# Four-layer graph network: the loops over pairs of edge groups in the attention stage, written out as straight code on all five engines

## The chip, the core and the metric

The kernel runs on one core of one Trainium2 chip. The metric is device time in microseconds (us) from the program's start to its end. Beside it there is one profiled execution, whose rows are quoted here. In it PE is TensorE's matmul, PEld its weight load, DVE is VectorE, ACT is ScalarE, POOL is GpSimd and SP is SyncE, which here only starts transfers; a "q" behind an engine's name (DVEq, SPq) is its sequencer, which fetches and hands out the instructions.

## What is computed

A graph of 6250 nodes (128 values each) and 206250 directed edges, sorted by destination, goes through four residual layers. Layers 0 and 1 average neighbours' rows and multiply by weights; layer 3 is a small MLP over edge statistics. The change is inside layer 2, three rounds of graph attention with four heads:

```python
def _gat_layer(x, src, dst, W_i, a_src_i, a_dst_i, b_i):
    h = (x @ W_i).reshape(n, H, C)
    es = jnp.einsum('nhc,hc->nh', h, a_src_i)
    ed = jnp.einsum('nhc,hc->nh', h, a_dst_i)
    e = es[src] + ed[dst]
    e = jnp.where(e > 0, e, NEG_SLOPE * e)
    m = jax.ops.segment_max(e, dst, num_segments=n)
    p = jnp.exp(e - m[dst])
    denom = jax.ops.segment_sum(p, dst, num_segments=n)
    alpha = p / denom[dst]
    msg = alpha[:, :, None] * h[src]
    return jax.ops.segment_sum(msg, dst, num_segments=n).reshape(n, H * C) + b_i
for i in range(3):
    x = jax.nn.elu(_gat_layer(x, src, dst, W[i], att_src[i], att_dst[i], bias[i]))
```

## The kernel before

The program is written per engine: each of the five blocks (`sync`, `gpsimd`, `scalar`, `tensor`, `vector`) is one instruction stream in the order of the source, and the engines meet only at semaphores (`wait_ge`, `then_inc`). No scheduler moves anything.

In the attention stage one *round* (`for n in range(LAYERS)`, three of them) first writes a table of 136-wide rows (`table`, in DRAM), one per node. Edges come in slots of 128. A *group* is 32 slots (`GROUP`), a round has 52 groups (`NG`), and two groups make a *pair*, since the buffers (`gathered`, `prob`, the flags) are double: an even group (b = 0) uses half 0, an odd one (b = 1) half 1. There are 26 pairs (`PAIRS`).

- **POOL** (lines 639 to 650) gathers: for each slot one indirect DMA (line 648) that fetches the 128 source rows of that slot out of `table` into `gathered`. That is 64 per pair, 1664 per round, 4992 in all. It does 8 of them, then waits (line 644) until PE has summed two more batches of the group that used the same half before. The first eight of group g + 2 so wait for batches 0 and 1 of group g.
- **DVE** (`dve_group`, line 1858) works through a group in eight batches of four slots. It rescales a running sum (`rescale`, line 1834), weighs rows by the softmax numerators (`weigh`, line 1842, two batches ahead), and adds PE's results to the accumulator (`add_batch`, line 1855). Between the batches it prepares the next group: its scores at m = 0 (`score_edges`, line 1771, which waits for that whole group to be gathered), scans for the segment maxima (lines 1781 to 1813), and the 0/1 matrices (lines 1751, 1756). In rounds 0 and 1 it also runs scans over the edge attributes for the last layer (lines 1517, 1519).
- **PE** (`pe_group`, line 1168) multiplies each slot's 0/1 matrix by its weighted rows (`sum_batch`, line 1164), turns scores and maxima, and does small score products (line 1092).
- **ACT** (`act_group`) copies the gather indices, takes the exponentials and stores edge scans. **SP** loads destination rows, flags and edge attributes.

Each engine has its own hardware loop over the pairs. POOL's covers all 26; on SP, ACT, PE and DVE it covers 25, and the last pair is written out behind it. In a loop the iteration is a register, so thresholds and slot offsets that depend on it are computed by register instructions. The loops before and after the attention stage, and those between its rounds (`over_groups`, `table_rows`, `store_rows`), are not touched by the change.

Of the kernel before, what the change touches and what calls it, by code (L numbers as in the profile page):

```python
# [84 lines left out]
def build_graph_network(nc, g, a, out):  # L85
# [23 lines left out]
    with ExitStack() as ctx:  # L109
# [269 lines left out]
        PAIRS = NG // 2  # L379
# [22 lines left out]
        def _(sp):  # L402
# [43 lines left out]
            def store_rows(i):  # L446
                sp.dma_start(table.rearrange("(t p) w -> p t w", p=P)[:, bass.ds(i * TG, TG), :],
                             H[:, bass.ds(i * TG, TG), :]).then_inc(table_stored, 16)
# [57 lines left out]
            def load_dst(slot):  # L506
                sp.dma_start(pick_t, dst_rows[bass.ds(slot, GROUP), :].unsqueeze(0).to_broadcast([P, GROUP, P])
                             ).then_inc(att.rows_loaded, 16)
# [14 lines left out]
            for n in range(LAYERS):  # L523
                load_dst(0)
                for b in range(2):
                    load_flags(b * GROUP, b)
                if n < STATS_LAYERS:
                    for q in range(2):
                        scan_loads(n, 0, q)
                sp.wait_ge(att.dst_scored, n * NG + 1)  # L530
                load_dst(GROUP)
                with sp.Fori(0, PAIRS - 1) as it:
                    for b in range(2):
                        slot = it * (2 * GROUP) + b * GROUP
                        sp.wait_ge(att.dst_scored, n * NG + it * 2 + b + 2)
                        load_dst(slot + 2 * GROUP)
                        sp.wait_ge(att.used, n * NG + it * 2 + b + 1)
                        load_flags(slot + 2 * GROUP, b)
                        if n < STATS_LAYERS:
                            for q in range(2):  # L540
                                scan_loads(n, it * 2 + b + 1, q)
                if n < STATS_LAYERS:
                    for q in range(2):
                        scan_loads(n, NG - 1, q)
                if n < LAYERS - 1:
                    with sp.Fori(0, NTG) as i:
                        sp.wait_ge(tab.rows, (n + 1) * NTG + i + 1 + FREE)
                        sp.wait_ge(tab.parts, (n + 1) * NTG + i + 1 + FREE)
                        store_rows(i)
# [13 lines left out]
        def _(pool):  # L563
# [71 lines left out]
            for n in range(LAYERS):  # L635
                pool.wait_ge(table_stored, (n + 1) * 16 * NTG)
                if n == 0:
                    pool.sem_inc(att.summed, 2 * NBATCH)
                with pool.Fori(0, PAIRS) as it:
                    for b in range(2):  # L640
                        pool.wait_ge(att.staged, n * (NG + 1) + it * 2 + b + 1)
                        for q in range(RNG):

                            pool.wait_ge(att.summed, (n * NG + it * 2 + b) * NBATCH + (q + 1) * (ROUND // BATCH))
                            pool.sem_inc(tick, 1)
                            for k in range(q * ROUND, (q + 1) * ROUND):
                                at = b * GROUP + k
                                pool.indirect_dma_start(gathered[:, at, :], None, table,  # L648
                                                        bass.IndirectOffsetOnAxis(staged_idx[:, at:at + 1], 0)
                                                        ).then_inc(att_gathered[n][b], 16)  # L650
                if n < LAYERS - 1:

                    if n == 0:
                        pool.sem_inc(n3.summed, FREE)
                    pool.wait_ge(n3.weighed, n + 1)
                    if n == STATS_LAYERS - 1:
                        for i in range(NTG):
                            pool.wait_ge(n3.summed, n * NTG + i + FREE)
                            pool.sem_inc(tick, 1)
                            own_rows(pool, n, i).then_inc(n3.own_ready, 1)  # L660
                            if i == 0:
                                for stored in st_stored:
                                    pool.wait_ge(stored, 32 * (SCANS // 2 + FREE))
                                pool.wait_ge(st.carried, 1)
                            node_stats(i)
                    else:
                        with pool.Fori(0, NTG) as i:
                            pool.wait_ge(n3.summed, n * NTG + i + FREE)
                            pool.sem_inc(tick, 1)
                            own_rows(pool, n, i).then_inc(n3.own_ready, 1)  # L670
# [4 lines left out]
        def _(act):  # L675
# [40 lines left out]
            def table_stage(k, first):  # L716

                over_groups(act, ((first, 2), (lambda i: table_out(k, i), 0), (lambda i: table_turned(k, i), 1)))
# [81 lines left out]
            for n in range(LAYERS):  # L800

                for b in range(2):
                    nc.scalar.copy(staged_idx[:, b * GROUP:(b + 1) * GROUP],
                                   src_of[:, b * GROUP:(b + 1) * GROUP]).then_inc(att.staged, 1)

                if n == 0:
                    for stored in st_stored:
                        act.sem_inc(stored, 32 * FREE)
                def stage(b, use, slot):
                    act.wait_ge(att_gathered[n][b], 16 * GROUP + use * (16 * GROUP))  # L810
                    nc.scalar.copy(staged_idx[:, b * GROUP:(b + 1) * GROUP],
                                   src_of[:, bass.ds(slot + 2 * GROUP, GROUP)]).then_inc(att.staged, 1)

                def act_exps(head, b):
                    act.wait_ge(att.shifted, head + 1)
                    nc.scalar.activation(prob[:, b, :, :], score[:, :, :], ACT.Exp).then_inc(att.prob, 1)
                    act.wait_ge(att.scale_rows, head + 1)
                    nc.scalar.activation(old_scale[:, :], bank[:, 3, SCALE_AT:SCALE_AT + HEADS], ACT.Exp
                                         ).then_inc(att.scale, 1)

                def act_group(it, b, head, ahead):
                    g = it * 2 + b
                    if ahead:
                        stage(1 - b, it + b, it * (2 * GROUP) + (b + 1) * GROUP)
                    if n < STATS_LAYERS:
                        scan_out(n, g, 0)
                    if head:
                        act_exps(n * NG + g + 1, 1 - b)
                    if n < STATS_LAYERS:
                        scan_out(n, g, 1)  # L830

                stage(0, 0, 0)
                act_exps(n * NG, 0)
                with act.Fori(0, PAIRS - 1) as it:
                    for b in range(2):
                        act_group(it, b, True, True)
                act_group(PAIRS - 1, 0, True, False)
                act_group(PAIRS - 1, 1, False, False)

                act.wait_ge(n3.scored, n + 1)  # L840
                nc.scalar.activation(att_w[:, 2:4, :, :], att_w[:, 2:4, :, :], ACT.Exp).then_inc(n3.weights, 1)
                if n == 0:
                    act.sem_inc(n3.elu, FREE)

                def exp_min(i):
                    act.wait_ge(n3.summed, n * NTG + i + 1 + FREE)
                    act.wait_ge(n3.elu, n * NTG + i + FREE)
                    act.sem_inc(act_tick, 1)
                    nc.scalar.activation(sq[:, :, :], H[:, bass.ds(i * TG, TG), 0:D], ACT.Relu, scale=-1.0)
                    act.drain()  # L850
                    nc.scalar.activation(sq[:, :, :], sq[:, :, :], ACT.Exp, scale=-1.0).then_inc(n3.weights, 1)

                if n < LAYERS - 1:
                    table_stage(n + 1, exp_min)
# [28 lines left out]
        def _(pe):  # L883
# [201 lines left out]
            for n in range(LAYERS):  # L1085
# [111 lines left out]
                turn_maxima(n * NG)  # L1197
                score_some(0, QG, GROUP, (n * NG + 1) * 2)
                spread_scale(n * NG)
                with pe.Fori(0, PAIRS - 1) as it:  # L1200
                    for b in range(2):
                        pe_group(it, b, True, True)
                pe_group(PAIRS - 1, 0, True, False)
# [39 lines left out]
        def _(dve):  # L1243
# [498 lines left out]
            for n in range(LAYERS):  # L1742
# [159 lines left out]
                carries(n * NG, 0)  # L1902
                last_scans(n * NG, 0)
                shift_scores(n * NG, 0, 0)
                with dve.Fori(0, PAIRS - 1) as it:
                    for b in range(2):
                        dve_group(it, b, True, True)
                dve_group(PAIRS - 1, 0, True, False)
# [161 lines left out]
```

## Time and profile before

| | us |
|---|---|
| Median of 3 runs (lowest, highest) | 9554.08 (9553.32, 9557.27) |
| The profiled execution, its own time | 9555.71 |
| Its span, first instruction to last | 9553.8 |
| Busy: DVE | 6364.0 (67%) |
| Busy: PE | 5680.6 (59%) |
| Busy: POOL | 5587.7 (58%) |
| Busy: ACT | 1058.2 (11%) |

Register, branch, semaphore and DMA-issuing work of a sequencer is not counted as busy, so an engine at 58% can still be one that never rests. An engine's "idle before" is the time between two of its instructions, and the name behind the arrow is what ended it; "issue" means that the profile shows nothing it waited for.

### The profile page before, as it was taken

The page shows a single profiled execution, that of the slowest core. Times are in us where ns is not written, and L with a number is a line of the kernel's source. Part 1 is how long each engine was busy: PE and PEld are TensorE (multiplying, and loading weights), DVE is VectorE, ACT ScalarE, POOL GpSimd, SP SyncE. Part 2 cuts the span into 40 slices and gives each one's busy share as a digit, 9 for nine tenths or more (in the row PEclk, how much of TensorE's full clock was granted, in tenths as well). Part 3 has the DMA queues.
Part 4 walks back from the last instruction along what each step waited for, and adds up shares of the span by engine and source line. Part 5 has one row for each costly group of instructions (what it writes and reads, how often), then busy time and mean ns, then how long its engine had stood idle before and what let it go on. Part 6 is the DMA issues. An engine that isn't in the chain of part 4 may idle for free.

```text
span 9553.8 us, 136929 instructions
## 1 busy us (share of the span) xinstructions
PE 5680.6 (59%) x34288; PEld 4531.3 (47%) x34289; DVE 6364.0 (67%) x13643; ACT 1058.2 (11%) x1906; POOL 5587.7 (58%) x5192
## 2 busy tenths in 40 slices
PE   4999799945555555555455555555535454545456
PEld 3777556644444444444344444444424444444444
DVE  6888711137777777777577777777746666666666
ACT  3555300020000000001000000000010000000003
POOL 2000100147777777774677777777667777777770
PEclk9999899965555555555555555555555555555558
DMA  3333245324444344342334434444322323232321
GB/s 102 141 134 141 101 175 189 127 62 108 108 110 117 108 110 118 108 109 69 106 108 110 117 108 109 118 109 109 99 63 76 81 77 81 76 81 76 82 76 32
DMA packets 601371, 986.89 MB, mean 103 GB/s; under 512 B 331106, under 2 KB 455043, under 8 KB 561523
## 3 DMA queue, kind: packets, MB, share of 16 engines
q1 hardware_dynamic: 217540, 544.34, 16.3%
q0 software_dynamic: 163760, 357.05, 15.9%
q10 hardware_dynamic: 219648, 81.82, 3.2%
q14 instruction: 396, 3.24, 0.1%
q8 instruction: 27, 0.44, 0.0%
HBM read 758.42 MB, written 224.34 MB: 103 GB/s over the span
## 4 chain that ended last, share of the span: by engine, by line
POOL 25%; PE 23%; issue 17%; DVE 16%; DVEq 14%; DMA 3%; ACT 1%; POOLq 0%; SPq 0%; ACTq 0%
POOL arena L648 23%; PE bank L941 13%; DVEq L1246 10%; DVE acc L1855 7%; PE bank L1164 4%; DMA arena<-row_table,staged_idx 3%; PE bank L966 2%; DVEq L1847 2%; DVE arena L1842 2%; DVE arena L1756 2%; DVEq L1855 1%; DVE arena L1811 1%; PE bank L1229 1%; PE bank L947 1%; DVE arena L1804 1%
## 5 line engine op out<-in xcount | busy, mean ns | idle before, releaser
L648 POOL DMA_INDIRECT arena<-row_table,staged_idx x4992 | 5299.5, 1062 | 1715.7 <-issue 1585.9
L1164 PE MATMUL bank<-arena 128*128 128x136 f32 x9984 | 2497.6, 429 | 1459.5 <-DVE acc L1855 973.6
L1164 PEld LDWEIGHTS bank<-arena 128*128 128x128 f32 x9984 | 2178.6, 313 | 1646.9 <-DVE acc L1855 1089.7
L1855 DVE TENSOR_TENSOR acc<-acc,bank 128x136 f32 x4992 | 1476.9, 296 | 1015.7 <-issue 813.3
L941 PE MATMUL bank<-arena 128*128 128x385 bf16 (+1 forms) x7546 | 1342.4, 327 | 49.5 <-DVE arena L1621 33.0
L596 POOL TENSOR_TENSOR arena<-acc,node_stat 128x896 f32 x14 | 24.5, 1746 | 1720.2 <-POOLq L608 955.0
L941 PEld LDWEIGHTS bank<-arena 128*128 128x128 bf16 x7546 | 711.0, 98 | 476.5 <-DVE arena L1621 33.3
L1842 DVE TENSOR_TENSOR arena<-arena,prob 128x528 f32<-128x528 f32 x1248 | 847.4, 698 | 5.8 <-issue 4.6
L1756 DVE TENSOR_TENSOR arena<-col,dst_local 128x1024 f32<-128x1024 f32 x624 | 767.4, 1231 | 0.0
L1490 DVE TENSOR_TENSOR arena<-key_line,x_mem 128x1024 bf16<-128x1024 bf16 x1216 | 690.5, 626 | 65.2 <-PE bank L966 51.5
L1092 PE MATMUL bank<-dst_parts,arena 128*128 x4992 | 536.8, 185 | 289.4 <-issue 220.3
L1092 PEld LDWEIGHTS bank<-dst_parts,arena 128*128 128x128 bf16 x4992 | 434.2, 108 | 401.8 <-issue 352.1
L744 ACT CAST arena<-bank 128x784 bf16<-128x784 f32 x608 | 507.0, 848 | 409.6 <-PE bank L966 409.6
L1104 PE MATMUL bank<-ident,x_mem 96*128 96x96 f32 x1664 | 314.7, 370 | 389.1 <-DVE x_mem L1519 389.1
L1120 PE MATMUL bank<-ident,arena 128*32 128x128 f32 x624 | 130.7, 350 | 580.4 <-DVE arena L1774 580.0
L754 ACT COPY x_mem<-bank 128x384 f32<-128x384 f32 x416 | 178.9, 482 | 2656.3 <-PE bank L1104 2656.3
L1104 PEld LDWEIGHTS bank<-ident,x_mem 96*128 96x128 f32 x1664 | 259.7, 223 | 449.5 <-issue 449.5
L1771 DVE TENSOR_TENSOR arena<-arena 128x128 f32<-128x128 f32 x156 | 61.0, 391 | 597.6 <-DMA arena<-row_table,staged_idx 596.8
L1142 PE MATMUL bank<-ident,arena 32*128 32x32 f32 x624 | 94.0, 288 | 440.7 <-DVE arena L1813 440.7
L1120 PEld LDWEIGHTS bank<-ident,arena 128*32 128x32 f32 x624 | 58.8, 114 | 622.1 <-DVE arena L1774 609.6
L966 PE MATMUL bank<-arena 128*128 128x98 bf16 x4864 | 322.0, 210 | 0.0
L966 PEld LDWEIGHTS bank<-arena 128*128 128x128 bf16 x4864 | 288.5, 99 | 61.9 <-DVE arena L1490 0.2
(354 smaller groups left out, 5029.8 us busy)
## 6 DMA issues: line engine op xcount, KB each, us to landing
arena<-dst_rows SPq DMA_DIRECT2D x156, 1024.0 KB, 5.5
cell_rows<-arena SPq DMA_DIRECT2D x76, 1568.0 KB, 5.1
arena<-cell_rows SPq DMA_DIRECT2D x76, 1568.0 KB, 6.5
arena<-row_table,staged_idx POOLq DMA_INDIRECT x4992
edge_stats<-x_mem ACTq DMA_DIRECT2D x416, 192.0 KB, 2.8
x_mem<-in_edge_attr SPq DMA_DIRECT2D x208, 192.0 KB
x_mem<-segment_flags SPq DMA_DIRECT2D x416, 96.0 KB
arena<-change_rows SPq DMA_DIRECT2D x312, 64.0 KB
```

Source lines behind the costliest of these rows:

```text
L648: pool.indirect_dma_start(gathered[:, at, :], None, table, bass.IndirectOffsetOnAxis(staged_idx[:, at:at + 1], 0)).then_inc(att_gathered[n ...
L744: nc.scalar.copy(out_cells[:, u * UNIT:(u + 1) * UNIT, :, :], pair[:, :, 0:CELLS].rearrange("p s (j d) -> p s j d", d=SUB)).then_inc(d0.ke ...
L941: mm = pe.matmul(bank[:, 4 + b, 0:width], cell_mem[f][:, j * P:(j + 1) * P], Hp[:, j, 0:width], start=j == 0, stop=j == NT - 1)
L966: mm = pe.matmul(bank[:, at_bank, at_col:at_col + CELLS], hot_src[:, r // PAIR, :, r % PAIR], hot_cell[:, r // PAIR, :, r % PAIR], start=T ...
L1092: mm = pe.matmul(bank[:, 2, k * PARTS * HEADS:(k + 1) * PARTS * HEADS], pick_t[:, k, :], dst_parts[:, bass.ds(at[k % 4], PARTS * HEADS)], ...
L1104: mm = pe.transpose(bank[:, m, c * 2 * EA:(c + 1) * 2 * EA], scanned[:, c * P:(c + 1) * P], ident[0:2 * EA, 0:2 * EA])
L1164: mm = pe.matmul(region(k)[:, 0:ROW], pick[:, k, :], gathered[:, b * GROUP + k, :], start=True, stop=True)
L1246: dve.drain()
L1490: made = dve.tensor_tensor(hot[:, first:first + UNIT // PAIR, :, :], key_line[:, 0:width * PAIR].rearrange("p (c t) -> p c t", t=PAIR).uns ...
L1756: dve.tensor_tensor(pick[:, q * ROUND:(q + 1) * ROUND, :], col_index.unsqueeze(1).to_broadcast(shape), dst_local[:, bass.ds(slot + q * ROU ...
L1842: dve.tensor_tensor(batch_rows, batch_rows, prob[:, b, :, m * BATCH:(m + 1) * BATCH].rearrange("p h s -> p s h").unsqueeze(3) .to_broadcas ...
L1855: done = dve.tensor_tensor(row, row, region(m * BATCH + k), ALU.add)
```

## The change

The `Fori` over pairs becomes a Python `range` on each engine. The instructions of each iteration are then written out in the program, 25 or 26 times per round, with the iteration as a constant in every semaphore threshold, slot offset and DRAM address. The work, its order on each engine and the semaphores stay.

```diff
@@ -529,7 +529,7 @@
                 load_dst(GROUP)
-                with sp.Fori(0, PAIRS - 1) as it:
+                for it in range(PAIRS - 1):
                     for b in range(2):
@@ -636,7 +636,7 @@
                     pool.sem_inc(att.summed, 2 * NBATCH)
-                with pool.Fori(0, PAIRS) as it:
+                for it in range(PAIRS):
                     for b in range(2):
@@ -831,7 +831,7 @@
                 act_exps(n * NG, 0)
-                with act.Fori(0, PAIRS - 1) as it:
+                for it in range(PAIRS - 1):
                     for b in range(2):
@@ -1197,7 +1197,7 @@
                 spread_scale(n * NG)
-                with pe.Fori(0, PAIRS - 1) as it:
+                for it in range(PAIRS - 1):
                     for b in range(2):
@@ -1902,7 +1902,7 @@
                 shift_scores(n * NG, 0, 0)
-                with dve.Fori(0, PAIRS - 1) as it:
+                for it in range(PAIRS - 1):
                     for b in range(2):
```

How the instructions stand, in two places. First DVE, where one pass over a pair ends and the next begins (round 0). Before, the last matrices of the odd group, then the loop's counter and its branch back to the top, which is the first row of the second piece:

```order
L1855 ISA
L1855 TENSOR_TENSOR acc<-acc,bank 128x136
L1756 ISA
L1756 TENSOR_TENSOR arena<-col,dst_local 128x1024
L1905 REGISTER_ALU
L1905 COMPARE_AND_BRANCH
```

```order
L1828 TENSOR_LOAD offsets
L1832 ISA
L1834 ISA [waits att_scale]
L1834 TENSOR_TENSOR acc<-acc,old_scale 128x132
L1842 TENSOR_TENSOR arena<-arena,prob 128x4x132 [waits att_prob]
```

Of the change, at the same place:

```order
L1855 ISA
L1855 TENSOR_TENSOR acc<-acc,bank 128x136
L1756 TENSOR_TENSOR arena<-col,dst_local 128x1024
L1828 TENSOR_LOAD offsets
L1834 ISA [waits att_scale]
L1834 TENSOR_TENSOR acc<-acc,old_scale 128x132
L1842 TENSOR_TENSOR arena<-arena,prob 128x4x132 [waits att_prob]
```

The branch and the register instructions are gone, the rest stands as before. DVE's stream grows from 2,211 to 17,691 such rows (equal neighbours are one row), PE's from 1,599 to 13,804.

Then POOL, at the start of a round. Before:

```order
L639 UNCONDITIONAL_BRANCH [waits table_stored]
L639 ISA
L644 ISA [waits att_staged]
L648 DMA arena<-row_table,staged_idx 128x136 [waits att_summed]
L648 DMA arena<-row_table,staged_idx 128x136 x7
L644 REGISTER_ALU
L648 DMA arena<-row_table,staged_idx 128x136 [waits att_summed]
L648 DMA arena<-row_table,staged_idx 128x136 x7
```

And of the change:

```order
L648 DMA arena<-row_table,staged_idx 128x136 [waits table_stored,att_staged,att_summed]
L648 DMA arena<-row_table,staged_idx 128x136 x7
L648 DMA arena<-row_table,staged_idx 128x136 [waits att_summed]
L648 DMA arena<-row_table,staged_idx 128x136 x7
```

POOL's waits stay in front of the same gathers; what computed their thresholds is gone.

## Rows read from the trace of the kernel before

**Rows 1.** Groups by line, round 0 (first), round 1, round 2: POOL's gathers.

```profile
line engine op names shapes xcount | busy us, mean ns | idle before us <-releasers
L648 POOL DMA_INDIRECT arena<-row_table,staged_idx x1664 | 1786.5, 1074 | 594.2 <-issue 546.8 <-PE bank L1164 47.4
...
L648 POOL DMA_INDIRECT arena<-row_table,staged_idx x1664 | 1759.0, 1057 | 595.8 <-issue 522.5 <-PE bank L1164 73.3
...
L648 POOL DMA_INDIRECT arena<-row_table,staged_idx x1664 | 1754.0, 1054 | 525.8 <-issue 516.6 <-PE bank L1164 9.1
```

**Rows 2.** Line 648 in each round: duration min/median/max, first and last start.

```profile
L648 POOL DMA_INDIRECT arena<-row_table,staged_idx x1664: 938/944/2394, 2078.1 to 4403.3; - x185
...
L648 POOL DMA_INDIRECT arena<-row_table,staged_idx x1664: 938/944/2347, 4559.8 to 6881.8; - x185
...
L648 POOL DMA_INDIRECT arena<-row_table,staged_idx x1664: 940/944/2323, 7071.8 to 9331.9; - x185
```

**Rows 3.** Waits of POOL by round: total us, times, longest us.

```profile
POOL arena L648 <- PE bank L1164: 47.4, 48, 2.9
...
POOL arena L648 <- PE bank L1164: 73.3, 53, 2.9
...
POOL arena L648 <- PE bank L1164: 9.1, 30, 0.3
```

**Rows 4.** Timeline, DVE, PE and POOL at a turn of the loop, round 0.

```profile
3140.88 1.22 DVE L1756 TENSOR_TENSOR arena<-col,dst_local 128x1024 f32<-128x1024 f32 x1
...
3145.22 0.30 DVE L1834 TENSOR_TENSOR acc<-acc,old_scale 128x132 f32 x1 [3.12 <-issue]
...
3146.27 3.99 PE L1164 MATMUL bank<-arena 128*128 128x136 f32 x16 [3.50 <-DVE arena L1842]
...
3148.51 0.94 POOL L648 DMA_INDIRECT arena<-row_table,staged_idx  x1 [0.30 <-issue]
3151.09 0.94 POOL L648 DMA_INDIRECT arena<-row_table,staged_idx  x1 [1.65 <-PE bank L1164]
```

**Rows 5.** Timeline, DVE and POOL inside the same pass, round 0.

```profile
3096.70 0.30 DVE L1834 TENSOR_TENSOR acc<-acc,old_scale 128x132 f32 x1 [0.19 <-issue]
...
3104.34 0.94 POOL L648 DMA_INDIRECT arena<-row_table,staged_idx  x1 [0.30 <-issue]
...
3106.94 0.39 DVE L1771 TENSOR_TENSOR arena<-arena 128x128 f32<-128x128 f32 x1 [4.63 <-DMA arena<-row_table,staged_idx]
```

**Rows 6.** Timeline, DVE and POOL at a turn of the loop, round 2.

```profile
8108.61 0.30 DVE L1834 TENSOR_TENSOR acc<-acc,old_scale 128x132 f32 x1 [5.19 <-issue]
...
8113.76 0.94 POOL L648 DMA_INDIRECT arena<-row_table,staged_idx  x1 [0.30 <-PE bank L1164]
```

**Rows 7.** Waits of DVE by round: before the rescaling, and for the gathers.

```profile
DVE arena L1771 <- DMA arena<-row_table,staged_idx: 160.5, 51, 18.0
DVE acc L1834 <- issue: 77.8, 50, 3.2
...
DVE arena L1771 <- DMA arena<-row_table,staged_idx: 160.9, 48, 26.6
DVE acc L1834 <- issue: 78.0, 50, 3.3
...
DVE arena L1771 <- DMA arena<-row_table,staged_idx: 255.4, 51, 17.8
DVE acc L1834 <- issue: 130.8, 50, 5.6
```

**Rows 8.** DMA queues that carry instructions: whole span, then round 0 alone.

```profile
q14 instruction: 396, 3.24, 0.1%
q8 instruction: 27, 0.44, 0.0%
...
q14 instruction: 123, 1.01, 0.1%
q8 instruction: 4, 0.07, 0.0%
```

**Rows 9.** Instruction queue from 2150 to 2240 us, and PE's one sequencer-side wait there.

```profile
q8 instruction: 3, 0.05, 0.3%
...
PE bank L1092 <- issue: 2.6, 6, 0.5
```

**Rows 10.** Round 0: DVE's drains, line 1855; busy us (x instructions) of PE, PEld, DVE, ACT, POOL.

```profile
L1246 DVEq DRAIN  x2065: 10/300/2396, 2088.3 to 4401.9; - x188
...
L1855 DVEq FUSED_REGOPS  x1604: 46/46/53, 2143.3 to 4401.6; - x179
...
2078.00:4404.00 2326.00, 1237.63 (x6402) 1047.40 (x6402) 1702.88 (x3543) 121.43 (x354) 1786.24 (x1664) 0.55 0.41 112
```

## The prediction

> **What bounds the kernel now.** By the page's busy shares DVE leads with 67% and POOL has only 58%, so a reader might begin with DVE. I read the groups by line for each attention round first. A round's 1664 gathers on POOL are busy for 1786.5, 1759.0 and 1754.0 us [rows 1], while POOL's gathering lasts from 2078.1 to 4403.3, from 4559.8 to 6881.8 and from 7071.8 to 9331.9 us [rows 2]: 2326, 2323 and 2261 us with the last gather's own 0.94. The timeline says what fills the rest: each gather stands 0.30 us behind the one before, at steady pace too, where it waits for nothing [rows 4, 5, 6]. 1664 x 0.30 is 499 us. Busy plus these gaps is 2286, 2258 and 2253 us, which leaves 40, 65 and 8 us. So POOL is the pacemaker of 6,910 of the 9,554 us: one gather takes its median 0.94, or longer, and 0.30 of gap, and POOL hardly ever stands. What can be won is what POOL still waits for.
>
> The waits of POOL name that: its gathers waited for PE's sums 47.4 us in 48 times in round 0, 73.3 in 53 times in round 1, 9.1 in 30 times in round 2 [rows 3]. Each of these holds the normal 0.30 as well. Net that is 47.4 - 48 x 0.30 = 33.0 us, 73.3 - 53 x 0.30 = 57.4 us, and 0.1 us; the three rounds' rests of 40, 65 and 8 are the same numbers plus about 7 of rounding of the 0.30.
>
> Where the waits sit is in the timeline at a turn of the loop. DVE ends line 1756 at 3142.10 and starts the rescaling only at 3145.22, after 3.12 us in which the profile shows nothing it waits for; then it weighs, PE sums from 3146.27 to 3150.26, and 0.83 us later, at 3151.09, POOL starts a gather that had stood 1.65 us instead of 0.30 [rows 4]. In the middle of the same pass the same rescaling comes after 0.19 us [rows 5]. The total of this wait is 77.8, 78.0 and 130.8 us in 50 times a round [rows 7]; 25 of each 50 are the normal 0.19, so a turn costs (77.8 - 4.8)/25 = 2.9 us in rounds 0 and 1 and (130.8 - 4.8)/25 = 5.0 us in round 2, about 2.8 and 4.9 over the normal one.
>
> What is it? A round's loop turns 25 times on DVE, and the instruction queue q14 carries 123 packets in round 0, near 5 per pass, while q8 carries 4 in the whole round [rows 8]. So an engine with the small queue fetches its loop body anew in each pass, and stands at the branch back. The Trainium skill has a rule for this (Runtime: NRT & Kernel Launch, Instruction fetch mechanics): fetching runs ahead only in a straight line, and a taken branch to a page that is not at hand costs a fetch. The trace agrees, with 2.8 us for a turn.
>
> **The change part by part.** *The branch on DVE.* 75 turns go, 25 a round. DVE gains 2.8 x 50 + 4.9 x 25 = 262 us of its own time. What of it reaches the end is what POOL waited because of it. In round 2 that is nothing: DVE stood 5.19 us at the turn and POOL's gather still came after its 0.30 [rows 6]; there DVE only waits longer for the gathers (255.4 us now [rows 7]). In rounds 0 and 1 it is 33.0 + 57.4 us. Per turn that is 1.3 and 2.3 us, less than the 2.8 that DVE is early by, so all of it can go: **-90.4 us**.
>
> *What is late next.* DVE must still be fast enough. From scoring one group (3106.94 [rows 5]) to the end of the first two sums of that group, with the turn, it is 3150.26 - 3106.94 = 43.3 us [rows 4]; without the turn's 2.9, about 40.4. Then 0.83 to POOL, 32 gathers (half of a pair; POOL's own pair is (1786.5 + 499)/26 = 87.9 us in round 0 and 86.8 in round 1, so 44.0 and 43.4), and about 1.7 from the end of the last gather (3104.34 + 0.94 [rows 5]) to the scoring. This ring is 40.4 + 0.83 + 44.0 + 1.7 = 86.9 us for two groups, against 87.9 for POOL alone; in round 1 it is 86.3 against 86.8. POOL stays ahead, by little. Single gathers last up to 2.4 us [rows 2], so now and then the ring will win: I take back 0.1 to 0.2 us per pair in 50 pairs, **+7 us**.
>
> *Gathers of another length.* The gathers of rounds 0 and 1 do the same beside the same DVE work, and differ by 1786.5 - 1759.0 = 27.5 us. This hangs only on which DVE work a gather falls beside, and the change shifts that. Both rounds could come to rest at round 2's 1754.0 (-37 us) or at round 0's 1786.5 (+28 us). I take **0** and keep both ends for the range.
>
> *Register instructions.* On POOL they cost nothing now: a gather behind a threshold that is computed comes 0.30 us after the one before, like any other (8113.76 [rows 6]). On DVE, PE, ACT and SP the cover is POOL's pace. In the 55 to 65 us of DVE work behind a round's last gather nothing changes, since the last pair was straight code already. **0**; if POOL's cover is gone it is a gain, never a loss.
>
> *Instruction traffic.* All five engines now stream. As DMA load it is nothing: now 3.7 MB of 987 MB, and DVE fetches no more than in the loop, since it fetched every pass anew. The question is whether a straight run stands at a new block. The nearest rows say no. DVE takes 5 packets a pass and shows one stall a pass; the other 4 are free. Between 2150 and 2240 us, as PE runs straight into its loop, q8 brings 3 packets, and PE's unexplained waits there are 2.6 us in 6, the longest 0.5 [rows 9]. The lower bound is 0. The upper bound is the turn's 2.8 us for each block that POOL fetches. DVE's round 0 is at least 3543 busy instructions, 2065 drains and 1604 register steps of line 1855 [rows 10] in 123 packets, so 59 or more to a packet; POOL's round is 1664 gathers and 208 semaphore steps, so at most 32 packets, 95 in three rounds, 266 us. I take **0**, with the rows.
>
> For PE a row of before shows no fetch inside the loops (4 packets in round 0 [rows 8]). The Trainium skill (Advanced Engine Details and Errata, ISA Cache) gives TensorE four times the instruction memory of the others, which fits, and means that PE now loses a loop that it held whole; the sum by that page changes only if its fetches stall.
>
> Sum: -90.4 + 7 = -83 us, against the profiled execution's 9555.7: 9472. That execution lies 1.6 above the median of the three runs, so the forecast is **9470 us**, 0.9% less.
>
> **The rivals.**
>
> *A: The ring takes over.* Without the turn, DVE and PE are the next limit at 86.9 against 87.9 us and 86.3 against 86.8. If I have the ring too short by 1 us per two groups, it and not POOL sets rounds 0 and 1, and 50 x 1 us come back: 9520. For it: the margin is under 1%. Against it: DVE loses register steps too, and it still waits for gathers 4.63 us in a pass of round 0 [rows 5].
>
> *B: All of DVE's stall comes off.* Read plainly, the skill's rule promises the 262 us, so 9292. Rows 6 speak against it: the largest stall of all moves POOL by nothing.
>
> *C: Straight code stalls, slower than before.* If POOL stands at each new block as DVE stands at the branch, that is up to 266 us on the engine that sets the pace, less the 83 gained: 9738. It decides from 30 such stalls, one per 2.6 pairs. For it: POOL and PE have never streamed in these rounds. Against it: DVE's four free packets of five, and rows 9.
>
> *D: The two cancel.* POOL or PE stand at some blocks only, 20 to 35 times 2.8 us: within 0.2%, about 9550.
>
> *E: The change does nothing.* The instruction order above shows the branches gone, and rows 4 tie a wait to one of them; I see 1 in 100.
>
> **How the numbers follow.** Forecast 0.72 (9430 to 9510, from -37 and +28 us of gather length and 0 to 15 of ring), A 0.12, B 0.02, C 0.07, D 0.06, E 0.01. 0.2% is 19 us, about what a measurement of this kernel can tell from no change. Faster: 0.72 + 0.12 + 0.02 = 0.86; same: D and E, 0.07; slower: C, 0.07. The range goes down to 9425 and up to 9530, which takes in A and leaves C, D, E and B outside.
>
> **What would show it.** In the profile after: no L1834 wait over 1 us except at a round's start; POOL's waits for L1164 down to near 0.30 each, so under 10 us net in rounds 0 and 1; round 2's gathers still lasting 2261 us; DVE's waits for the gathers up, in round 2 to about 255 + 123 = 378 us; q8 from 27 packets to over a hundred, q14 down from 396. Each gather still 0.30 behind the last. It is wrong if POOL shows "issue" gaps of 2 us or more spread evenly (C, D), or if its waits for L1164 stay at tens of us (A).

## The result: 1.8% slower, and the profile after

The changed kernel takes 9728.89 us (median of 3 runs, 9720.95 to 9731.02) against 9554.08: a ratio of 1.0178, 95% interval 1.0164 to 1.0192. The forecast was 9470 us, faster. The profiled execution's span is 9719.1 us, 165.3 more than before's 9553.8.

One thing must be known for all that follows: the kernel before ("the loop kernel") ran again beside every group of experiments, and its median was 9558.83 us in one group, as above (the quick level), and 10316.95, 10320.19, 10495.26 and 10312.29 in the four others (the slow level). Ratios are always to the loop kernel of the same group.

POOL's gathers by round (groups by line; rounds 0, 1, 2), beside [rows 1]:

```profile
L648 POOL DMA_INDIRECT arena<-row_table,staged_idx x1664 | 1880.4, 1130 | 561.2 <-issue 506.5 <-POOLq L638 54.3 <-PE bank L1164 0.3
...
L648 POOL DMA_INDIRECT arena<-row_table,staged_idx x1664 | 1881.2, 1130 | 538.0 <-issue 505.7 <-DMA row_table<-arena 31.1 <-PE bank L1164 1.2
...
L648 POOL DMA_INDIRECT arena<-row_table,staged_idx x1664 | 1796.5, 1080 | 526.3 <-issue 503.4 <-DMA row_table<-arena 19.5 <-PE bank L1164 3.4
```

The same 1664 gathers are busy for 93.9, 122.2 and 42.5 us more, 258.6 in all; the mean of one rises from 1074, 1057 and 1054 ns to 1130, 1130 and 1080. Their waits for PE's sums, the thing that the change was forecast to win, are gone: 0.3, 1.2 and 3.4 us, all of it in normal gaps of 0.3, against 47.4, 73.3 and 9.1 [rows 3]. The gathering of the rounds, beside [rows 2]:

```profile
L648 POOL DMA_INDIRECT arena<-row_table,staged_idx x1664: 940/945/2340, 2076.5 to 4462.8; - x185
...
L648 POOL DMA_INDIRECT arena<-row_table,staged_idx x1664: 940/945/2307, 4617.5 to 7004.6; - x185
...
L648 POOL DMA_INDIRECT arena<-row_table,staged_idx x1664: 940/944/2360, 7194.6 to 9497.0; - x185
```

From first to last start that is 2386.3, 2387.1 and 2302.4 us, against 2325.2, 2322.0 and 2260.1. The median of one gather has hardly moved (945 ns). So not all gathers are slower: a part of them is much longer.

The waits of DVE and POOL in round 0, beside [rows 3, 7]:

```profile
POOL arena L648 <- issue: 506.5, 1662, 0.3
DVE arena L1771 <- DMA arena<-row_table,staged_idx: 299.0, 51, 17.9
...
DVE acc L1834 <- issue: 9.4, 50, 0.2
POOL arena L648 <- PE bank L1164: 0.3, 1, 0.3
```

The rescaling (line 1834) waits 0.19 us each time: no turn is left, 77.8 us have become 9.4. The longest unexplained gap of POOL is 0.3 us, so POOL stands at no new block of code. DVE waits for the gathers 299.0 us where it waited 160.5. DVE is ahead, and POOL alone sets the pace.

The timeline at a former turn of the loop, round 0, beside [rows 4]:

```profile
3531.22 1.22 DVE L1756 TENSOR_TENSOR arena<-col,dst_local 128x1024 f32<-128x1024 f32 x1
3531.58 1.67 POOL L648 DMA_INDIRECT arena<-row_table,staged_idx  x1 [0.30 <-issue]
3532.62 0.30 DVE L1834 TENSOR_TENSOR acc<-acc,old_scale 128x132 f32 x1 [0.19 <-issue]
...
3533.64 3.97 PE L1164 MATMUL bank<-arena 128*128 128x136 f32 x16 [1.28 <-DVE arena L1842]
```

The 3.12 us before the rescaling are 0.19. And a gather that starts while line 1756 runs lasts 1.67 us and not 0.94. That leads to the cause.

The instruction queues of the whole span, beside [rows 8]:

```profile
q8 instruction: 192, 3.15, 0.1%
q14 instruction: 284, 2.33, 0.1%
```

**Which gathers are longer.** Here the gathers are grouped by the DVE operation that runs as they start. Beside most operations a gather lasts 0.94: beside line 1855, which reads one of its two inputs from PSUM (`bank`), none of 803 in the kernel before is longer than 1.05 us. It lasts longer when DVE is in line 1751, 1756, 1842, or one of the scans (1517, 1519, 1783, 1811), and then it mostly ends about 0.82 us after that operation's end (0.75 behind a scan). If two such operations follow each other without a pause, it is held through both. The largest part of what the change adds comes from one spot, where line 1751 starts up to 30 ns after a gather. The kernel before there (the timeline, round 1):

```profile
5641.30 0.17 DVE L1796 TENSOR_TENSOR cross<-carry_b,masks 4x32 f32<-4x32 f32 x1
5641.38 0.95 POOL L648 DMA_INDIRECT arena<-row_table,staged_idx  x1 [0.30 <-issue]
5641.40 0.73 DVE L1751 TENSOR_SCALAR arena<-arena,part_index 128x2048 bf16<-128x2048 bf16 x1
5642.07 0.69 DVE L1842 TENSOR_TENSOR arena<-arena,prob 128x528 f32<-128x528 f32 x1
5642.64 0.94 POOL L648 DMA_INDIRECT arena<-row_table,staged_idx  x1 [0.30 <-issue]
```

The changed kernel at the same spot of a pass (round 0):

```profile
3740.48 0.17 DVE L1796 TENSOR_TENSOR cross<-carry_b,masks 4x32 f32<-4x32 f32 x1
3740.57 2.19 POOL L648 DMA_INDIRECT arena<-row_table,staged_idx  x1 [0.31 <-issue]
3740.58 0.74 DVE L1751 TENSOR_SCALAR arena<-arena,part_index 128x2048 bf16<-128x2048 bf16 x1
3741.24 0.69 DVE L1842 TENSOR_TENSOR arena<-arena,prob 128x528 f32<-128x528 f32 x1
...
3743.06 0.94 POOL L648 DMA_INDIRECT arena<-row_table,staged_idx  x1 [0.30 <-issue]
```

Line 1751 starts 20 and 10 ns behind the gather, as good as the same, and yet the gather lasts 0.95 us in the one and 2.19 in the other, 0.83 past the end of line 1842. Of the gathers that start up to 30 ns ahead of line 1751, none of 99 is longer than 1.3 us in the kernel before, and all of 127 are in the changed one. The distances are of the same size (10 to 29 ns before, 5 to 25 after), so the starts that the profile shows don't tell who is first. What differs ahead of line 1751 is one step of DVE's sequencer, in the kernel before:

```profile
L1879 DVEq FUSED_REGOPS  x75: 46/46/46, 2173.0 to 9256.9; - x75
L1879 DVEq ALU_OP  x75: 40/40/40, 2219.2 to 9300.5; - x75
```

It computes the threshold of `att.rows_loaded` from the loop's register, the first row for one group of a pass and the second for the other. With constants it does not exist, so that nothing of the sequencer stands between lines 1796 and 1751. So the theory is: **DVE's straight code has line 1751 ready earlier, it takes from POOL what both need, and POOL is the engine that sets the pace.**

The Trainium skill (SBUF — State Buffer, Who interferes with whom) has this as a rule: VectorE, in its 2-port modes or (against a GpSimd instruction that reads SBUF) with two inputs in SBUF, and GpSimd take a shared pair of ports as a lock for a whole instruction, and the order of issue decides which of them stands. The trace agrees in kind: lines 1756 and 1842 have two inputs in SBUF and lengthen gathers, line 1855 with one in PSUM does not, and line 1751 is not slowed (0.73 and 0.74 us) while the gather is. The same section tells of a probe in which `tensor_tensor` did not stall a DMA; lines 1756 and 1842 are `tensor_tensor`, and here the gather beside line 1756 lasts 1.67 us, so the measurement decides. The prediction had not weighed this rule. That it is the ports, and not something else that the two share, no run here shows.

### The profile page after: what moved, and what is told of

It reads as the page before. It is cut to its first block, busy times and chain, and to the rows that moved or that the text cites. A ratio compares the mean times of both kernels' runs of the same rounds, so it can differ in the third digit from the quotient of the medians.

```text
span 9719.1 us, 123202 instructions
## 1 busy us (share of the span) xinstructions
PE 5666.2 (58%) x34288; PEld 4547.5 (47%) x34288; DVE 6347.4 (65%) x13643; ACT 1050.8 (11%) x1906; POOL 5843.9 (60%) x5192
## 4 chain that ended last, share of the span: by engine, by line
DVE 28%; PE 20%; DVEq 19%; POOL 14%; issue 12%; DMA 5%; ACT 1%; POOLq 0%; SPq 0%; ACTq 0%
DVEq L1246 16%; POOL arena L648 13%; PE bank L941 13%; DVE acc L1855 12%; DMA arena<-row_table,staged_idx 4%; DVE arena L1756 3%; PE bank L966 2%; DVEq L1855 2%; DVE arena L1842 2%; DVE arena L1811 2%; DVE arena L1781 2%; DVEq L1847 1%; DVE arena L1804 1%; DVE x_mem L1517 1%; PE bank L1229 1%
## 5 line engine op out<-in xcount | busy, mean ns | idle before, releaser
L648 POOL DMA_INDIRECT arena<-row_table,staged_idx x4992 | 5558.0, 1113 | 1625.5 <-issue 1515.7
L1164 PEld LDWEIGHTS bank<-arena 128*128 128x128 f32 x9984 | 2200.7, 316 | 1486.2 <-issue 1485.7
L1120 PE MATMUL bank<-ident,arena 128*32 128x128 f32 x624 | 161.1, 414 | 1043.3 <-DVE arena L1774 1043.3
L1771 DVE TENSOR_TENSOR arena<-arena 128x128 f32<-128x128 f32 x156 | 60.7, 389 | 1063.8 <-DMA arena<-row_table,staged_idx 1063.8
L1092 PE MATMUL bank<-dst_parts,arena 128*128 x4992 | 516.0, 185 | 191.5 <-issue 126.8
```

Source lines behind the costliest of these rows:

```text
L648: pool.indirect_dma_start(gathered[:, at, :], None, table, bass.IndirectOffsetOnAxis(staged_idx[:, at:at + 1], 0)).then_inc(att_gathered[n ...
L1092: mm = pe.matmul(bank[:, 2, k * PARTS * HEADS:(k + 1) * PARTS * HEADS], pick_t[:, k, :], dst_parts[:, bass.ds(at[k % 4], PARTS * HEADS)], ...
L1164: mm = pe.matmul(region(k)[:, 0:ROW], pick[:, k, :], gathered[:, b * GROUP + k, :], start=True, stop=True)
```

## The experiments

Theory P (above): the 258 us are made by DVE's missing step, whatever the other engines do. Rivals: straight code on the other engines (POOL's own stream, or traffic) slows the gathers; or the lost stall at the turn lets gathers and DVE meet more often. The measure is the busy time of line 648 (loop kernel 5299.5, changed kernel 5558.0); for the changed kernel it turned out nearly the same at both levels (5552.5 to 5563.7), while the totals are not. Times named in the early expectations start from 9554 us and were given before any group had met the slow level; where later ones speak of "a chip of the 10317 sort", they mean the slow level.

**Which engine.** `e1_dve_straight`: only DVE's loop is written out.

```diff
-                with dve.Fori(0, PAIRS - 1) as it:
+                for it in range(PAIRS - 1):
```

> Only DVE's loop is written out; SP, POOL, ACT and PE keep theirs. Theory L (DVE's instructions now fall differently against POOL's gathers, and more gathers last long): all of the change is DVE's, so about 9720 us, POOL's L648 busy about 5550 us and no waits of POOL for L1164. Theory S (the instruction streams of POOL and PE lengthen the gathers or hold POOL up): with POOL and PE in loops the loss goes and the gain stays, about 9470 us, L648 busy about 5300.

`e2_all_but_dve`: the same edit on SP, POOL, ACT and PE, with DVE left in its loop.

> All loops but DVE's are written out. Theory L: DVE's turn of the loop and its register steps are as before, so 9554 us within 0.2%, L648 busy about 5300, POOL's waits for L1164 about 130 us, DVE's L1834 waits about 287 us. Theory S: the loss is here, 9640 to 9810 us, with L648 busy about 5550.

Measured, e1 and then e2, from the groups by line:

```profile
L648 POOL DMA_INDIRECT arena<-row_table,staged_idx x4992 | 5552.7, 1112 | 2031.0 <-issue 1578.1
```

```profile
L648 POOL DMA_INDIRECT arena<-row_table,staged_idx x4992 | 5303.7, 1062 | 2440.9 <-issue 1702.8
```

DVE's straight code alone makes the gathers long (5552.7), the other four engines' does nothing to them (5303.7). At the spot of line 1751, all 114 such gathers are long in e1 and none of 76 in e2. That part of the theory stands. The totals were a surprise: 10151.96 and 10310.13 us against 10316.95 for the loop kernel, ratios 0.9843 [0.9820, 0.9867] and 0.9993 [0.9981, 1.0005]. On the slow level the same long gathers go with a faster kernel.

**The stall or the step.** `e3_stall_back` gives the changed kernel a pause of DVE at every turn again:

```diff
+        pad_cell = sb("pad_cell", [1, 1])
...
                         dve_group(it, b, True, True)
+                    for _ in range(11):
+                        dve.memset(pad_cell[:, :], 0.0)
+                        then()
```

> The changed kernel, with 11 one-element memsets and drains on DVE at the end of each pair, about 2.8 us that stand in for the branch's stall. Theory L with the stall as its cause (the pause at the turn moved the gathers out of the way of DVE's instructions): 9550 to 9600 us, and POOL waits for L1164 again in rounds 0 and 1. Theory L with the small register steps as its cause: the gathers stay long, 9700 to 9800 us. Theory S: the same as the changed kernel or more, since the stream is longer.

Gathers 5535.1 us, 10125.49 us in all (0.9811 [0.9786, 0.9836]). The pause gives back 23 us of the gathers' 258, and at the spot of line 1751 all 97 gathers are long: it is not what had kept them short. (It is a pause of 2.13 us in most passes, where the loop's turn took 3.1 in rounds 0 and 1, so the turn is not copied exactly.)

`e4_drain_after_pick` parts lines 1751 and 1842 by a drain:

```diff
                             build_pick_t(0)
+                            then()
...
                             build_pick_t(1)
+                            then()
```

> The changed kernel, with a drain on DVE behind each line 1751 in the group, so that it doesn't run straight into line 1842 and POOL can start its gather between them. Theory L: the gathers that lasted 2.19 us there last about 1.45, and about 100 to 160 us come back: 9570 to 9630 us. Theory S: no gain, 9720 to 9740 us.

Gathers 5304.6 us, as in the loop kernel; 10177.91 us in all (0.9867 [0.9844, 0.9890]). `f3_drain_again` is the same kernel in the next group.

> The drain behind line 1751 once more, beside the changed kernel on its own chip. Theory L: L648 busy 5300 us as in the first run of this kernel, and with POOL as the pacemaker 9460 to 9500 us, about 1% under the loop kernel. If DVE's extra drains decide instead: over 9554.

Gathers 5308.8, ratio 0.9875 [0.9859, 0.9892]. The drain doesn't change who is first (a gather at the spot still lasts 1.56 to 1.59 us), it ends the hold between the two operations.

`f2_step_before_pick` puts back one step of the sequencer and no more:

```diff
                             dve.wait_ge(att.rows_loaded, ...)
+                            dve.sem_inc(dve_tick, 1)
                             build_pick_t(0)
```

> The changed kernel with one semaphore step on DVE's sequencer in front of the first line 1751 of a group, where the loop kernel had a register step of 46 ns. Theory L-step (line 1751 is queued too early since that step is gone and takes the port from a gather that starts 10 to 20 ns before it; line 1842 then follows without a pause): POOL wins that race again, gathers of 2.19 us vanish, L648 busy near 5300 us, 9470 to 9520 us. Theory L-stall (it was the pause at the turn of the loop that kept the gathers short): no gain, 9700 to 9740.

Its timeline at the spot:

```profile
3768.73 0.17 DVE L1796 TENSOR_TENSOR cross<-carry_b,masks 4x32 f32<-4x32 f32 x1
3768.81 0.95 POOL L648 DMA_INDIRECT arena<-row_table,staged_idx  x1 [0.30 <-issue]
3768.83 0.73 DVE L1751 TENSOR_SCALAR arena<-arena,part_index 128x2048 bf16<-128x2048 bf16 x1
```

All 120 gathers at this spot are short again, where in `f1_changed_again`, the changed kernel in the same group, 122 of 122 are long. Line 648 is busy for 5367.1 us against f1's 5563.7. The one step so accounts for 197 of the 258 us, 152 of them at the spot itself; nothing else in the program differs.

> The changed kernel itself, for comparison on the same chip. On a chip without the many waits marked remote, 9729 us with POOL's L648 busy at about 5558 us.

f1 took 10093.76 us, 0.9783 [0.9767, 0.9800]; f2 10219.14, 0.9906 [0.9890, 0.9923]. `f4_split_pick` cuts line 1756 in halves with a drain between (on top of e4), so that it holds POOL half as long at a time.

> The drain kernel, with each line 1756 (1.22 us) cut into two halves with a drain between, so that a gather that meets one waits for a half at most. Theory L: the gathers that lasted 1.40 us beside line 1756 last 1.0 to 1.1, L648 busy 5150 to 5250 us, 9380 to 9450 us as far as DVE has room for about 1.5 us more a group. Against it: DVE becomes the bound and it is 9500 or more.

Gathers 5151.1 us, 150 below the loop kernel's, 10196.03 in all (0.9883 [0.9865, 0.9901]). The mechanism can be used on purpose; on the slow level it buys no time.

**A third group**, again on the slow level (loop kernel 10495.26), to repeat the changed kernel, the drain, the split and e2.

> The changed kernel as it is, third time, as the base of this call. Two chips so far gave 10317 and 10320 us for the loop kernel, with spells of 0.70 us a sequencer step on DVE and PE, and 0.978 for the changed one; the first chip gave 9554 and 1.018. Theory (gathers get 258 us longer, and what shows in the total is only whether POOL sets the pace): L648 busy 5550 to 5570 us on any chip; the ratio is 1.018 where the loop kernel takes about 9554 and 0.978 where it takes about 10317. Rival (the length of the gathers is not what decides, the chips differ in how they run the straight code): the ratio is something else on a chip of either sort.

> The changed kernel with DVE's drain behind line 1751 (build_pick_t). L648 busy 5300 to 5310 us on any chip, 255 less than the changed kernel. Theory: where the loop kernel takes about 9554, POOL's pace sets the time and the 255 us come off: 9729 - 255 = 9474 us, ratio 0.992, faster than both. Where the loop kernel takes about 10317, POOL waits for PE and the drain gives nothing: 0.987 as before. Rival (the ring of DVE and PE takes over at once without the long gathers): 9520 to 9560, ratio 0.997 to 1.000 on a chip of the first sort.

> The drain kernel with line 1756 in two halves and a drain between. L648 busy 5150 us (412 less than the changed kernel). If POOL's pace set everything, a chip of the 9554 sort would show 9729 - 412 = 9317, ratio 0.975; theory: the ring of DVE and PE (about 87 us a pair, 78 pairs, and the stages around) ends at about 9470 to 9520, so the ratio is 0.991 to 0.997 and POOL's waits for line 1164 take the rest. On a chip of the 10317 sort 0.988 again.

> All loops straight but DVE's. L648 busy 5300 to 5305 us on any chip, as in the loop kernel. Theory: where the loop kernel takes about 9554 it stays within 0.3% of it (9530 to 9580), since DVE's turn and DVE's order beside the gathers are the old ones. Rival (straight code on POOL, PE, ACT or SP costs too): over 9600. On a chip of the 10317 sort 0.999 again.

| | line 648 busy, us | total, us | ratio [95%] |
|---|---|---|---|
| `h1_changed_third` | 5552.5 | 10241.89 | 0.9773 [0.9753, 0.9793] |
| `h2_drain_third` (edit of e4) | 5323.7 | 10310.51 | 0.9826 [0.9802, 0.9849] |
| `h3_split_third` (edit of f4) | 5174.9 | 10303.09 | 0.9824 [0.9805, 0.9843] |
| `h4_all_but_dve_second` (edit of e2) | 5314.1 | 10391.03 | 0.9912 [0.9893, 0.9931] |

The gathers came as expected within 25 us. Of the ratios only h1's did. h4's 0.9912 lies outside e2's interval, so the slow level isn't one fixed thing. Nor is it shown to belong to a chip: this group and the next, quick one are recorded with the same chip number.

**A fourth group**, on the quick level, with the loop kernel's own trace.

> The kernel before, unchanged, for its trace on a chip like the last three. Theory (spells in which DVE's and PE's sequencers take 0.70 us a step, more of them with loops, so that DVE and PE and not POOL set the pace there): ratio 1.000 within 0.003; L648 busy 5300 us as on the first chip; over 150 register steps of DVE above 0.5 us (none on the first chip) where the time is near 10317, and POOL's waits for PE's sums, with the ones marked remote, at 700 to 1000 us net, against 90 there. Rival (another cause of the 760 us, such as slower gathers or transfers): no slow steps, and L648's busy time or the DMA waits carry the difference.

> The changed kernel beside it. L648 busy 5550 to 5565 us. Theory: POOL waits for PE's sums 250 to 350 us net and fewer than 60 slow steps on DVE; ratio 0.978 where the loop kernel takes over 10300, 1.018 where it takes 9554. Rival (the ratio follows neither the gathers nor POOL's waits): POOL's net waits differ from the loop kernel's by less than 200 us.

k1 repeats the kernel before (9558.23 us, 1.000 [0.999, 1.001]), k2 the result (9721.33, 1.0170 [1.0153, 1.0187]). Their gathers, k1 first:

```profile
L648 POOL DMA_INDIRECT arena<-row_table,staged_idx x4992 | 5301.5, 1062 | 1715.8 <-issue 1586.8
```

```profile
L648 POOL DMA_INDIRECT arena<-row_table,staged_idx x4992 | 5555.9, 1113 | 1625.6 <-issue 1517.0
```

This closes the account. Busy +254.4, idle before -90.2, together +164.2; the spans are 9554.1 and 9718.2, so +164.1. Nothing of the 1.7% is left for any engine's work outside the gathers, and the granted clock of TensorE (0.639 and 0.634) is no cause either: PE is busy for 5687.0 and 5676.5 us. By the operations beside the gathers, 155 of the 254 us lie at line 1751 with 1842 (80 us in k1, 235 in k2), 73 at line 1519, 39 at lines 1756 with 1818 and 52 at line 1842 alone, while 66 went at line 1517: once some gathers are longer, the later ones meet other operations of DVE.

`k3_loop_with_drain` is the loop kernel with e4's drains.

> The loop kernel with DVE's drain behind line 1751. In the loop kernel POOL's gather already starts ahead of line 1751, so theory says the drain does not change the length of the gathers at those places: L648 busy 5290 to 5310 us against 5300, and the time within 0.5% of the loop kernel's. Rival (the drain helps the gathers anywhere, by spacing line 1751 from 1842): busy 5150 to 5250 us.

Gathers 5336.1 us, 9602.79 in all (1.0045 [1.0029, 1.0062]). So a drain doesn't shorten gathers as such: where POOL already is first, as at 100 of 100 such spots here, it only costs. The gathers are 26 us above the upper end of what was expected, the time 0.05% inside its end, and the rival's 5150 to 5250 is far off. Here too the gathers carry the total: +34.6 busy and +10.8 idle, for a span 46.7 longer than k1's.

**A fifth group** was to put the two cures on the quick level. It met the slow one (loop kernel 10312.29).

> The changed kernel with DVE's drain behind line 1751, hopefully on a chip where the loop kernel takes 9555 to 9559 as in the last call. L648 busy 5300 to 5310 us. Theory: POOL's pace sets the time there, and of the changed kernel's 9721 the 255 us of longer gathers come off, less what the ring of DVE and PE now keeps: 9470 to 9520, ratio 0.991 to 0.996. Rival (the ring takes over at once; the loop kernel with the same drain lost 0.45%): 9540 to 9600, ratio 0.998 to 1.004. On a chip of the 10317 sort 0.983 to 0.988.

> The changed kernel with one semaphore step of DVE before line 1751. L648 busy 5360 to 5370 us, 195 less than the changed kernel. Theory: 9721 - 195 = 9526, less the few us in which POOL did not set the pace: 9520 to 9545, ratio 0.996 to 0.999. Rival (the length of the gathers is not what the time hangs on): over 9650. On a chip of the 10317 sort 0.991.

> The drain kernel with line 1756 in two halves and a drain between. L648 busy 5150 us. Theory: now the ring of DVE and PE is what ends last, since two more drains and operations are in it: 9450 to 9520, ratio 0.989 to 0.996, with POOL waiting for PE's sums 100 to 200 us net. Rival (POOL's pace still sets all): 9317 to 9350, ratio 0.975 to 0.979. On a chip of the 10317 sort 0.982 to 0.988.

| | line 648 busy, us | total, us | ratio [95%] |
|---|---|---|---|
| `m1_drain_fourth` | 5329.3 | 10161.55 | 0.9857 [0.9840, 0.9873] |
| `m2_step_fourth` | 5368.9 | 10231.71 | 0.9927 [0.9911, 0.9944] |
| `m3_split_fourth` (edit of f4) | 5183.7 | 10201.52 | 0.9897 [0.9881, 0.9914] |

They repeat e4, f2 and f4. That a cure would bring the quick level near the forecast's 9470 is only argued from the account above, and not shown.

**Why the slow level turns the sign.** k2 and h1 are the same program on the two levels, so their traces can be laid side by side instruction by instruction. Hardly any duration differs (PE's busy time by 1 us, DVE's by 15, POOL's by 11; the granted clock is 0.629 and 0.634). The 519 us are gaps. On PE there are 452 us more ahead of line 1164, 173 ahead of 1142 and 145 ahead of 1092, and 345 less ahead of 1120. A spell that shows the kind, h1's PE at small products for which the profile shows it waiting for nothing:

```profile
2176.65 0.17 PE L1092 MATMUL bank<-dst_parts,arena 128*128 x1 [2.63 <-issue]
2178.05 0.17 PE L1092 MATMUL bank<-dst_parts,arena 128*128 x1 [1.23 <-issue]
2179.45 0.17 PE L1092 MATMUL bank<-dst_parts,arena 128*128 x1 [1.23 <-issue]
2180.85 0.17 PE L1092 MATMUL bank<-dst_parts,arena 128*128 x1 [1.23 <-issue]
```

And k2's at the same products:

```profile
2137.44 0.54 PE L1092 MATMUL bank<-dst_parts,arena 128*128 x4 [0.32 <-issue]
2138.31 0.53 PE L1092 MATMUL bank<-dst_parts,arena 128*128 x4 [0.33 <-issue]
```

One product takes its 0.17 us on both, but they come every 1.40 us instead of four in 0.54. DVE's sequencer has such spells too. Of its register steps, normally 40 or 46 ns, those above 0.5 us are none in the kernel before, the changed one, k1, k2 and k3; 44 to 101 in the slow runs with DVE straight (e3: 31); and 333 and 339 in e2 and h4, where DVE is in its loop. POOL then waits for PE. h1's waits, where "remote" marks a release whose record the trace lacks:

```profile
POOL arena L648 <- remote: 372.1, 144, 3.8
...
POOL arena L648 <- PE bank L1164: 75.1, 57, 3.4
```

h4's:

```profile
POOL arena L648 <- remote: 401.4, 151, 3.9
POOL arena L648 <- PE bank L1164: 254.4, 81, 6.5
```

Less 0.30 for each, that is 387 and 586 us, where k2's are normal gaps (3.4 us in 11). So on the slow level it is DVE and PE that often set the pace. It is argued from this, and not shown, that DVE's straight code is there worth what it saves DVE, while longer gathers fall in part into waits; the loop kernel itself has no trace on the slow level, and h4 stands for it. h4 against h1: busy -238.4, idle +358.3, +119.9 together, of the 133.2 us between their spans (10369.9 and 10236.7). What makes the spells stays open: no experiment takes them away, and the instruction queues carry the same packets in h1 and k2 (192 and 284).

## Why the prediction was wrong

**The branch on DVE: right in size, not shown as to its cause.** -90.4 us were forecast. Line 1834's unexplained wait fell from 287.2 to 29.1 us in all, POOL's waits for line 1164 to normal gaps, and POOL's idle time before its gathers from 1715.7 to 1625.5, which is -90.2. But POOL became slower too, and by an estimate that alone would have ended nearly all its waits. In rounds 0 and 1 of the changed kernel's trace the first gather of an even group starts 5.2 us (median) after the sums that it needs; a gather that has to wait starts 0.83 us after them. If a turn's 2.8 us came back ahead of those sums, 47 of the 50 would still not wait. So the turn's gain may be nothing beside gathers this long, and its hitting the forecast is in part luck.

**What is late next: not tried.** The ring of 86.9 us never met a POOL of 87.9, since POOL became slower: (1880.4 + 499)/26 = 91.5 us a pair in round 0. POOL waits for PE nowhere. The +7 us stay untested on the quick level, and rival A with them.

**Gathers of another length: this step failed.** It said that the length "hangs only on which DVE work a gather falls beside". That names the right kind of cause and misses the decisive one: at the spot above the same work stands beside the gather, up to 30 ns behind its start, and it lasts 0.95 or 2.19 us by who is first. And it took 0, with -37 and +28 as its ends, from the spread between the rounds of a kernel that has the same register step in every group. Those rounds differ in where gathers and DVE meet; in none of them does DVE win at that spot (99 of 99 gathers there are short). The edit changes who wins, which no row of before showed from both sides. The measured term is +258.5 us (+254.4 in k1 and k2), nine times the upper end. A hint was there: 2394 ns for the longest gather [rows 2] tells that DVE can hold one for 1.45 us. One such hold a group would have been 156 x 1.25, the 2.19 - 0.94 of the spot above, or 195 us. That this is close to f2's 197 is chance: 127 gathers were held so, which makes 158 us.

**Register instructions: half right.** "0; if POOL's cover is gone it is a gain, never a loss" is what f2 disproves. POOL loses nothing by its own steps, as forecast. DVE lost a step of 46 or 40 ns a group, and to put one step back took 197 us off POOL's gathers.

**Instruction traffic: right.** 0 was taken. q8 went from 27 to 192 packets, q14 from 396 to 284, and POOL's longest unexplained gap in a round is 0.3 us. Rival C, the one on the slower side, gave 9738 us and the time came out at 9729; that nearness is chance. C's mark would have been gaps of 2 us and more, and there are none. The slower side was right for a reason that stood in the sum as 0.

**Rival B** (all of DVE's stall comes off) is refuted by DVE's waits for gathers, up from 596.8 to 1063.8 us. **What would show it** came true but for two lines: waits of line 1834, POOL's waits, the queues and the gaps of 0.30 all did; "round 2's gathers still lasting 2261 us" did not, with 2303, nor did DVE's waits for them in round 2 at about 378 us, with 432.1. Neither of the two signs of being wrong appeared, since both looked at POOL's gaps and none at the length of its gathers.

The sum with the measured term: -90.2 + 258.5 = +168 us, against +165.3 in the span. The ring's term is 0 in it.

## What to carry to other kernels

Where POOL's gathers set the pace, look at which DVE operations they start beside, and price an edit on DVE by what it does to their length, even one that only removes register steps. A term that is taken as "stays the same" because it differs little between parts of one program has no bound from that, if the edit touches what all these parts have in common. And a kernel with two levels of time can gain on one what it loses on the other: -2.2% and +1.8% here for the same edit, so a comparison should say on which it stands.

## What the runs showed of the hardware that I had not expected

- Who goes first between a gather and a DVE operation is not to be read from starts that differ by up to 30 ns. With a register step of 40 or 46 ns (or a semaphore step) ahead of line 1751 POOL won 99 of 99 and 120 of 120 times, without it DVE won 127 of 127, 122 of 122 and 114 of 114.
- The loss is one-sided. Where POOL is first, line 1751 still takes its 0.73 us; where DVE is first, the gather takes 2.19 instead of 0.94 us. The 1.25 us more are about the time of one more gather with its gap (0.94 + 0.30).
- The same program ran at 9558 and at 10312 to 10495 us, with nearly equal durations of single instructions and more gaps in PE's and DVE's streams, in spells in which a step of DVE's sequencer takes about 0.70 us.
